# Float32 products with whole weights in place of float32r products of split parts, in a transformer layer's feed-forward and attention output

## What is computed

```python
x = x + attn(layernorm(x)) @ Wo.T          # 16 heads of 16, window of 128 plus one global token
h = layernorm(x) @ (tern1 * scale1).T + gate * (layernorm(x) @ v.T @ fast_b.T @ u.T)
r = maximum(h, 0)                          # 8192 x 1024
out = x + (r * r) @ (tern2 * scale2).T     # back to 256
```

## Time and profile before

| | us |
|---|---|
| time, median of 3 runs (1153.77 to 1153.89) | 1153.78 |
| profiled execution, span from first to last instruction | 1152.4 |
| `stage_project`, to about | 183 |
| `stage_attend`, to about | 781 |
| `stage_feed` | the rest |
| mean granted TensorE clock, share of full speed | 0.994 |

### The profile page before, as it was taken

How to read it: one execution, slowest core, us unless ns; L and a number is a source line. 1 busy time by engine, 2 the same in 40 slices (tenths; PEclk the granted TensorE clock), 3 DMA queues, 4 the chain that set the end, 5 groups by cost and what they waited for, 6 DMA issues and landing times.

```text
span 1152.4 us, 26576 instructions
## 1 busy us (share of the span) xinstructions
PE 1126.9 (98%) x9115; PEld 785.0 (68%) x9115; DVE 979.5 (85%) x3169; ACT 843.4 (73%) x1513; POOL 706.8 (61%) x935
## 2 busy tenths in 40 slices
PE   9999997999999999999999999999999999999998
PEld 8888884455555555555555455558888988898887
DVE  7889857899889998899889999867888888888885
ACT  7989983788888888888788888875465546554654
POOL 3665565677778777887778877773344334433443
PEclk9999998999999999999999999999999999999999
DMA  6999897555555555545565554240232113211201
GB/s 199 295 296 281 257 266 168 114 131 118 137 133 122 132 125 136 132 115 137 126 138 130 114 138 108 68 139 29 74 102 64 56 55 102 64 55 56 74 20 37
DMA packets 158166, 145.24 MB, mean 126 GB/s; under 512 B 21564, under 2 KB 157776, under 8 KB 158032
## 3 DMA queue, kind: packets, MB, share of 16 engines
q1 hardware_dynamic: 158032, 143.54, 48.8%
HBM read 91.74 MB, written 50.95 MB: 124 GB/s over the span
## 4 chain that ended last, share of the span: by engine, by line
PE 73%; DVE 7%; issue 2%; ACT 1%; POOL 1%; DVEq 0%; POOLq 0%; ACTq 0%
PE e_psum L1549 15%; PE e_psum L1503 15%; PE e_psum L1527 14%; PE e_psum L1844 6%; PE e_psum L1846 5%; PE e_psum L1267 3%; PE e_psum L1825 3%; PE e_psum L1824 3%; DVE n_stats L142 2%; DVE f_x L1958 2%; PE e_psum L1829 1%; PE e_psum L255 1%; PE e_psum L254 1%; PE e_psum L253 1%; PE e_psum L1793 1%
## 5 line engine op out<-in xcount | busy, mean ns | idle before, releaser
L1665 DVE CUSTOM_DVE_ANT_0 a_masked<-e_psum,band 128x387 f32<-128x387 f32 (+1 forms) x1024 | 493.3, 534 | 58.8 <-PE e_psum L1503 55.8
L1622 ACT ACTIVATE a_weights<-e_psum 128x1024 f32<-128x1024 f32 (+1 forms) x512 | 398.0, 806 | 87.2 <-PE e_psum L1527 82.2
L1401 POOL TENSOR_SCALAR_AFFINE_SELECT a_weights<-a_weights 128x1024 f32<-128x1024 f32 x256 | 276.2, 1091 | 59.9 <-ACT a_weights L1622 58.7
L1503 PE MATMUL e_psum<-e_k,e_q 96*128 96x387 bf16 (+1 forms) x1024 | 281.4, 327 | 3.0 <-PEq L281 1.4
L1888 POOL TENSOR_TENSOR f_square<-f_relu 128x512 f32<-128x512 f32 x128 | 146.1, 1142 | 209.6 <-ACT f_relu L1877 198.6
L1527 PE MATMUL e_psum<-e_q,e_k 128*128 128x384 bf16 (+2 forms) x1408 | 255.6, 279 | 1.5 <-ACT a_weights L1622 1.1
L1549 PE MATMUL e_psum<-a_weights,a_v 128*17 128x384 f32 (+2 forms) x2816 | 195.8, 392 | 1.0 <-POOL a_weights L1401 1.0
L1527 PEld LDWEIGHTS e_psum<-e_q,e_k 128*128 128x128 bf16 x1408 | 129.0, 98 | 95.6 <-issue 39.5
L1503 PEld LDWEIGHTS e_psum<-e_k,e_q 96*128 96x128 bf16 x1024 | 100.4, 98 | 99.2 <-DVE a_max L1665 44.8
L1844 PE MATMUL e_psum<-w_w_t,f_square_hi 128*128 128x256 f32 x512 | 129.4, 287 | 5.6 <-DVE f_square_lo L1934 5.6
L1846 PE MATMUL e_psum<-w_w_t,f_square_lo 128*128 128x256 f32 x512 | 126.8, 282 | 0.0
(11 more groups left out here) (219 smaller groups left out, 2059.0 us busy)
## 6 DMA issues: line engine op xcount, KB each, us to landing
k_parts<-p_k_parts SPq DMA_DIRECT2D x48, 258.0 KB, 4.6
e_k<-k_parts SPq DMA_DIRECT2D x64, 193.5 KB, 3.6
e_k<-k_parts SPq DMA_DIRECT2D x192, 64.5 KB, 3.3
q_parts<-p_q_parts SPq DMA_DIRECT2D x48, 256.0 KB, 5.1
e_q<-q_parts SPq DMA_DIRECT2D x64, 192.0 KB, 3.7
e_q<-q_parts SPq DMA_DIRECT2D x192, 64.0 KB, 3.3
v_ones<-p_va SPq DMA_DIRECT2D x16, 544.0 KB, 5.9
p_x<-in_x SPq DMA_DIRECT2D x16, 512.0 KB, 6.3
```

Of the source, the lines that this page charges most:

```text
L1401: pool.affine_select(out=blocks, in_=blocks, compare_op=ALU.is_ge, fill=0.0, base=0, pattern=[[0, NQ // 2 * HEAD_COLS // P // CUT_STEP], [ ...
L1503: pe.matmul(sh.tile_bank(ux, j)[:, lo:hi], qw[ux.q][0:SLOT_ROWS, h, t * P:t * P + P], kt[ux.hq][0:SLOT_ROWS, h, start + lo:start + hi], st ...
L1622: act.activation(pe_w[:, us.upar, lo:hi], score[c % 2][:], ACT.Exp).then_inc(s_exp, 1)
L1665: dve.tensor_tensor_reduce(out=masked[:, ux.upar, h, t:t + hi - lo], in0=bank[:, lo:hi], in1=band[:, lo:hi], scale=1.0, scalar=NEG, op0=AL ...
```

## The change

Every product named above is replaced by single float32 products. The scales and the low-rank term move into the weights once: `diag1` and `mag_diag` are diagonal matrices of the scales, and the weight transposes of `pe_w1` and `pe_w2` become float32 products with them; `pe_w1` first adds (fast_b v gate) times u, in one float32 product of 16 rows, into the same bank. `pe_low_rank`, `pe_low`, `act_z_high`, `dve_z_low`, `pe_mag`, `act_mag`, `dve_low`, GpSimd's squares, all low parts and the scaling by `mag_row` are gone; the layout of memory is kept by unused tensors.

```diff
-            weights.pe_w1(pe, 0)
+            weights.pe_u(pe)
             pe.wait_ge(s_rv, 1)
             pe.transpose(turn_bank[0:B * H, 0:P], m_tok[:], ident[:]).then_inc(s_rpe, 1)
-            weights.pe_w1(pe, 1)
             pe.wait_ge(s_rv, 3)
             pe.matmul(over_bank[:, 0:B * H], ones[0:B * H, :], m_diag[:], start=True, stop=True).then_inc(s_rpe, 1)
-            idle_products(total_bank, 10)
+            weights.pe_w1(pe, 0)
+            weights.pe_w1(pe, 1)
...
     def pe_w1(self, pe, n):
         k, c = divmod(n, 2)
+        bank = self.ring[n]
         pe.wait_ge(self.s_tern1, MH)
+        pe.wait_ge(self.s_diag1, 2)
+        pe.wait_ge(self.s_pc, 4)
+        pe.matmul(bank[:], self.low_b[:, k * P:k * P + P], self.u_t[:, c * GT:(c + 1) * GT], start=True, stop=False,
+                  skip_group_check=True)
         for m in range(TB):
-            ins = pe.transpose(self.ring[(2 + n) % 4][:, m * P:m * P + P],
-                               self.w1_in[:, c * TB + m, k * P:k * P + P], self.ident[:])
+            ins = pe.matmul(bank[:, m * P:m * P + P], self.w1_in[:, c * TB + m, k * P:k * P + P],
+                            self.diag1[:, c * TB + m, :], start=False, stop=(m == TB - 1), skip_group_check=True)
         ins.then_inc(self.s_pt, 1)
...
-                    if ux and ux.n == 0 and j in (5, 7):
-                        weights.pe_u(pe, j // 2 - 2)
-                    if ux and ux.n == 0 and j in (9, 11, 13, 15):
-                        weights.pe_w2(pe, j // 2 - 4)
-                    if ux and ux.n == 1 and j == 3:
-                        weights.pe_mag(pe)
+                    if ux and ux.n == 0 and j in (5, 7, 9, 11):
+                        weights.pe_w2(pe, j // 2 - 2)
...
-                ins = three_pass(pe, self.attention_bank(q, c)[:, t * D:t * D + D],
-                                 [sh.ot_hi[:, k, part] for k in range(KT)], [sh.ot_lo[:, k, part] for k in range(KT)],
-                                 [w.wo_hi[:, k, :] for k in range(KT)], [w.wo_lo[:, k, :] for k in range(KT)])
+                for k in range(KT):
+                    ins = pe.matmul(self.attention_bank(q, c)[:, t * D:t * D + D], sh.ot[:, k, part], w.wo_t[:, k, :],
+                                    start=(k == 0), stop=(k == KT - 1))
...
-    def pe_ternary(self, pe, q, j):
+    def pe_hidden(self, pe, q, j):
+        if j == 0:
+            pe.wait_ge(self.s_xtc, q.g * KT + KT)
         wait(pe, self.s_r, q.g * MH + j - 1)
         for k in range(KT):
-            lhs = self.w.w1_t[:, k, j * P:j * P + P]
-            pe.matmul(self.h_bank[j % 2][:], lhs, self.sh.xt_hi[:, q.par, k, :], start=(k == 0), stop=False)
-            pe.matmul(self.h_bank[j % 2][:], lhs, self.sh.xt_lo[:, q.par, k, :], start=False, stop=False)
+            ins = pe.matmul(self.h_bank[j % 2][:], self.w.w1_t[:, k, j * P:j * P + P], self.sh.xt[:, q.par, k, :],
+                            start=(k == 0), stop=(k == KT - 1))
+        ins.then_inc(self.s_h, 1)
...
-                pe.matmul(y, sh.r2_hi[:, j % 4, part], self.w.w2_t[:, j, :], start=(j == 0 and t == 0), stop=False,
-                          skip_group_check=True)
-                ins = pe.matmul(y, sh.r2_lo[:, j % 4, part], self.w.w2_t[:, j, :], start=False, stop=(j == MH - 1),
-                                skip_group_check=True)
+                ins = pe.matmul(y, sh.r2[:, j % 4, part], self.w.w2_t[:, j, :], start=(j == 0 and t == 0),
+                                stop=(j == MH - 1), skip_group_check=True)
...
-        act.activation(sh.r[:, j % 4, :], self.h_bank[j % 2][:], ACT.Relu, scale=self.w.mag[:, j:j + 1]
-                       ).then_inc(self.s_r, 1)
+        act.activation(sh.r[:, j % 4, :], self.h_bank[j % 2][:], ACT.Relu).then_inc(self.s_r, 1)
         act.wait_ge(self.s_r, q.g * MH + j + 1)
-        act.activation(sh.r2_hi[:, j % 4, :], sh.r[:, j % 4, :], ACT.Square).then_inc(self.s_r2hi, 1)
+        act.activation(sh.r2[:, j % 4, :], sh.r[:, j % 4, :], ACT.Square).then_inc(self.s_sq, 1)
...
+    def dve_final(self, dve, q):
 
         for c in range(2):
-            if c == 0:
+            if c == 0 and q.g == G - 1:
                 dve.wait_ge(self.s_yfirst, 1)
             else:
                 dve.wait_ge(self.s_y, q.g * MH + MH)
             rows = self.x1_rows(q, c)
-            dve.tensor_tensor(self.scaled[:, c], self.y_bank[c][:], self.w.mag_row[:], ALU.mult).then_inc(self.s_yc, 1)
-            dve.wait_ge(self.s_yc, q.g * 2 + c + 1)
-            dve.tensor_tensor(rows, self.scaled[:, c], rows, ALU.add).then_inc(self.s_fin, 1)
+            dve.tensor_tensor(rows, self.y_bank[c][:], rows, ALU.add).then_inc(self.s_fin, 1)
```

More of the change, by code:

```diff
@@ L677, in _ @@
             weights.act_wo(act)
-            weights.act_w1(act, 0)
-            weights.act_w1(act, 1)
+            weights.act_u(act)
             act.wait_ge(s_rv, 4)
@@ L682, in _ @@
                            ).then_inc(s_rexp, 1)
+            weights.act_w1(act, 0)
+            weights.act_w1(act, 1)
         @block.vector
@@ L811, in _ @@
             ins.then_inc(s_rv, 1)
-            weights.dve_low(dve)
             for n in range((2 * G - weights.TERN2) // 2, 4 * KT):
@@ L1090, in pe_w2 @@
         pe.wait_ge(self.s_tern2, KT * (n + 1))
-        pe.wait_ge(self.s_pc, 4 + n)
+        pe.wait_ge(self.s_mag, 1)
+        if n >= 2:
+            pe.wait_ge(self.s_pc, 5 + n)
         for i in range(2):
             for m in range(KT):
[L1094 to L1102, removed]
-                ins = pe.matmul(self.ring[0][:, c * D + m * P:c * D + m * P + P], self.ones[:], self.mag_diag[:, m, :],
+                ins = pe.matmul(self.ring[n][:, i * D + m * P:i * D + m * P + P],
+                                self.w2_in[:, m, (2 * n + i) * P:(2 * n + i + 1) * P], self.mag_diag[:, m, :],
                                 start=True, stop=True)
@@ L1167, in __init__ @@
             over("fill1", [P, fill])
-            self.xt_hi, self.xt_lo = over("xt_hi", [P, 2, KT, GT], F32R), over("xt_lo", [P, 2, KT, GT], F32R)
+            self.xt = over("xt", [P, 2, KT, GT])
+            over("hole3", [P, 2 * KT * GT])
             over("fill2", [P, fill])
-            self.r, self.r2 = over("relu", [P, 4, GT]), over("square", [P, 4, GT])
+            self.r = over("relu", [P, 4, GT])
+            over("hole4", [P, 4 * GT])
             over("fill3", [P, fill])
@@ L1597, in _ @@
                 weights.act_w1(act, n)
-            for n in range(2):
-                weights.act_u(act, n)
             for n in range(4):
@@ L1776, in pe_turn_o @@
         for k in range(KT):
-            wait(pe, self.s_lo, (q.g - 2) * KT + k + 1)
-            if z and k == 0:
-                pe.wait_ge(self.s_zlo, z.g + 1)
+            wait(pe, self.s_xtc, (q.g - 2) * KT + k + 1)
             for t in range(TB):
@@ L1858, in act_o_high, with o_copies_dve, act_norm_copies @@
             wait(act, self.s_a, (q.g - 1) * 2 + 2)
-            act.activation(self.sh.ot_hi[:, k, :], self.t_bank[k][:], ACT.Copy).then_inc(self.s_oth, 1)
-    def act_norm_high(self, act, q):
+            act.activation(self.sh.ot[:, k, :], self.t_bank[k][:], ACT.Copy).then_inc(self.s_otc, 1)
+    def o_copies_dve(self, dve, q):
+        for k in range(KT):
+            dve.wait_ge(self.s_ot, q.g * KT + k + 1)
+            dve.tensor_copy(self.sh.ot[:, k, :], self.t_bank[k][:]).then_inc(self.s_otc, 1)
+    def act_norm_copies(self, act, q):
         for k in range(KT):
@@ L1995, in _ @@
             sp.wait_ge(feed.s_out[i], DMA * (G // 4 + (i == (G - 1) % 4)))
-    @block.gpsimd
-    def _(pool):
-        for g in range(G):
-            for j in range(MH):
-                feed.pool_squares(pool, Group(g), j)
     @block.tensor
@@ L2043, in body @@
             qa, qx, qf = at(0), at(LX), at(LF)
[L2044 to L2047 removed]
             for j in range(MH):
                 if qf:
[L2050 removed]
+                    feed.act_relu(act, qf, j)
+                if j == 1 and qf and qf.g == 0:
+                    sh.act_sums_read(act, Unit(UNITS - 1))
                 if j == 1 and qx:
```

241 lines of the change are left out of this document (59 added, 182 removed).

## The result

| | us |
|---|---|
| before, median of 3 | 1153.78 |
| changed, median of 3 (1316.33 to 1319.05) | 1316.92 |
| ratio, 95% interval | 1.1414 (1.1393 to 1.1434) |
| span, before and changed | 1152.4 and 1317.3 |

A forecast was written before the change was run, and what follows sets the result against it. The prediction took TensorE to bound the kernel. Its terms, 163.3 - 1.4 + 1.1 + 3.5 = +166.5 us, took the span from 1152.4 to 1318.9 us, so 1320 us measured, within 1301 to 1356.

The forecast's parts named there:

- A float32 product is two rows of two passes: New products in `stage_feed`: each streams four column times where float32r streams one; 0.438 us per 512-column row, 0.220 per 256.
- +163.3: `stage_feed`, from the attention product of group 1 to the last product: grows from 366.4 to 529.7 us.
- The low bound: Lowest row prices taken for float32 products: 0.424 us for 512 columns, 0.212 for 256; the stretch 17 us shorter.
- Nothing is late in place of the removed wait: `stage_feed`: output block 0's wait for `f_square_lo`, the present 0.4 us a group, goes and no other wait replaces it.
- The end of the kernel, -1.4 us: From the last product to VectorE's last sum: 2.3 us becomes 0.17 + 0.69, with one sum left for the second half.
- Work taken from VectorE, GpSimd and ScalarE is worth nothing: The operations removed from these engines are hidden behind TensorE, so they save no time.
- The weights: Readying scaled weights at the end of `stage_project` and in unit 0 of `stage_attend`: +1.1 and +3.5 us.
- +1.1: End of `stage_project`: `pe_w1` 0 and 1 replace the 10 idle products; 3.5 - 2.2 - 0.2 us.
- +3.5: Unit 0 of `stage_attend`: `pe_w1` 2 and 3 and `pe_w2` add time, `pe_mag` goes; between +2 and +8 us.
- Rivals A: Half rate: a float32 product's two rows pass once each; `stage_feed` -65 us, about 1090 us in all; 5 in 100.
- B: Weights not hidden: a float32 load of about 0.10 us stands before each row; +178 us, about 1498 us; 3 in 100.
- C: Float32 products cost one row and one pass, so ScalarE bounds `stage_feed` at 216 us; about 1005 us; 1 in 100.

The follow-up runs named there:

- the rounded run: All factors of the attention output and feed-forward products rounded to float32r, low parts left out, against the changed kernel: 1001.96 us, ratio 0.8681.
- the second run of the changed kernel: The changed kernel itself, with no further edit, measured again beside the kernel with padded low-rank factors: 1314.67 us, ratio 1.1399 to the kernel before.

## Why the prediction was right

- **A float32 product is two rows of two passes.** Right, to the row. The 0.438 and 0.220 us taken were 2% high: 0.429 and 0.216 were measured. With these the sum of the prediction is 512 x 0.429 + 1264 x 0.216 + 26 = 518.7 us, and the stretch took 518.4. Of the 11 us between +163.3 and +152.0 10 are this one term. A row's distance fits its stream at 0.833 ns a column and some 3 ns on top, whatever its columns: 110 ns at 128 (L487), 216 at 256, 429 at 512, where the stream alone is 107, 213 and 427. So the price a column of the short idle rows was too high for long ones. Why the strips of L1549 had given 0.85 was not tried. The low bound, from the slope of the means, was nearest.
- **The page that gives true FP32 four passes** (the Trainium skill, "FP8 and Floating Point Precision", TensorE Precision Notes) agrees: 0.84 ns a column and row, two rows a product. The factor of two for FP32_LOW_HIGH in "Perfetto Trace Analysis" (Engine Utilization) would hold at most for each of the two rows, as these traces show it.
- **Nothing is late in place of the removed wait.** Right: no wait of TensorE in the last stage. The end of the kernel, -1.4 us, was right too.
- **Work taken from VectorE, GpSimd and ScalarE is worth nothing.** Right: the rows of TensorE alone give the stretch to 0.3 us. And the rounded run shows from what point ScalarE would count: when TensorE streams little more than a third of this.
- **The weights.** Mechanism partly right, size wrong: +4.6 forecast, +12.8 measured. Two steps failed. The prediction let `pe_w1` 0 and 1 run at full clock where the idle products had stood (+1.1, with no range); the time from `pe_wo` to the first score tile grew by 6.4 us: 4.5 in these products and 2.0 in L580 behind them, which the prediction left at its length. Behind that tile +3.5 was forecast, +2 to +8, and +6.4 measured, inside the range but not as summed: the prediction had the low clock in unit 0 end where it ended before, at 187 us; in the changed kernel the eight rows of `pe_w2` at 199.36 still span 1.92 us, where 0.88 was summed. Both go when the low-rank products are padded: the path to the first score tile then costs 1.0 us over the kernel before, near the +1.1, and the whole one 1.6, less than the 4.6 forecast, since the low clock that the prediction kept in unit 0 is gone too.
- The +1.5 us ahead of `pe_wo` is not the change's: in the second run of the changed kernel `pe_wo` starts at 165.89.
- Rivals A, B and C fell: a row of 512 columns is 0.429 us apart from the next, not 0.23 or 0.54, and each product has two rows.

The total was within 4 us because an overestimate of 11 us and an underestimate of 8 us met, which is luck. The range would have held without that.

## What to carry to other kernels

Price a change of number format by passes, from rows of that format in the trace at hand: count the rows a product leaves, take the slope of their mean over the columns, and compare column times, not instructions. Here 4 for one float32 product against 2 for two float32r products or 3 for three: whoever can make one factor exact in float32r should stay with parts. And when the weight preparation is moved into products with few rows, look at the granted clock behind them, and try padding: here it gave 8.7 us.

## What the runs showed that was not expected

- Products of 16 rows let the clock fall while TensorE is busy without a gap: busy 4.00 of 4 us at a granted 0.50 (174 to 178 us, changed). The same products with zeros in the other 112 rows, 4.00 of 4 us at 1.00. The Trainium skill, "TensorE: Matmul & The Clock Gate" (Part 1), ties the gate to how busy TensorE has been. The profile's busy time does not tell the two kernels apart, neither in these stretches nor ahead of the fall: from 166 to 170 us TensorE is busy 3.34 us in the changed kernel's second run and 3.34 in the padded one, and from 170 to 178 us the first is at 0.50 and the other at 1.00. What in the few rows brings the level down is open.
- Even at a granted 1.00 such products went at a slower pace, and so did what followed: with idle products ahead, two rows of 512 columns took 1.05 us (171.70 to 172.75) and the next eight rows of 128 columns 1.09, against 0.86 and 0.89 when padded, 0.82 of the pace. What slows them is open.
- Float32 rows stream nearer to the full rate than float32r rows. 512 column times take 0.233 us as one float32r row of 512 columns and 0.216 us as one float32 row of 256. Why float32r pays 8% more was not tried.
